# Attention layer: forming the second output tile ahead of the encoder's transposes in position 5

## The chip, the cores and the metric

The kernel runs on one core of a Trainium2 chip. The metric is the device time of one execution in microseconds (us), less is better.

## What is computed

The reference is two transformer blocks one after the other, all in float32, on x of shape (8, 256, 512). The first block ("first layer") is a cross-attention block over channels with its own feed-forward part. The second block is the one that matters here; cut to its core, for eight batches of 256 tokens and 512 features with 16 heads of 32:

```python
ln_out = layernorm(hidden_states, ln1_s, ln1_b)
q, k, v = split(ln_out @ w_qkv + b_qkv)
x = hidden_states + merge_heads(attention(q, k, v, ltor_mask)) @ w_ao + b_ao
ln_out = layernorm(x, ln2_s, ln2_b)
q = ln_out @ w_q + b_q
k, v = split(encoder_states @ w_kv + b_kv)
x = x + merge_heads(attention(q, k, v, cross_mask)) @ w_co + b_co
return x + gelu(layernorm(x, ln3_s, ln3_b) @ w1 + b1) @ w2 + b2
```

The eight self-attentions and the eight cross-attentions are done by `attention_layer` (lines 932 to 1892); the last line is `network_layer` (lines 1895 to 2340).

## The kernel before

`attention_layer` runs 16 rounds, v = 0 to 15: rounds 0 to 7 are the self-attention of batch 0 to 7, rounds 8 to 15 their cross-attention. A round has eight positions p = 0 to 7, one for each unit of four heads by 128 queries. The order of every engine is written out by hand: each has a function `position(v, p)` that runs in a loop over v and p, and the engines meet through semaphores alone (`Signal`, with `need` and `wait_ge`).

TensorE, position p of round v (L1484): the scores of the unit two ahead (L1446), the transposes of this unit's probabilities (L1458, two banks of four), in even positions the weighing of the values of two earlier units (L1475, then two transposes of the widened divisors, L1481), and at last `fill(v, p)`, the matmuls of other rounds that the table `FILL` lists for that position (L1395). Work that stands in `fill` and matters here, by its name in the table and its shift in rounds:

- ("o", n, -1): output tile n (128 tokens by 512) of the round before, a matmul of the bias (L1388) and twelve of 512 columns (L1391, `by_token`).
- ("enc", n, 2): half n of the encoder's transposes for round v + 2, four transposes into one bank (L1368, `turn`). It exists only where v + 2 is a cross round, so in the rounds v = 6 to 13.
- ("q", 0, 2) and ("k", 0, 2): the first halves of the queries and keys of round v + 2, 24 matmuls each (L1379, `project`), in positions 6 and 7. The keys wait for both low parts of the encoder (`enc_low`), the queries for the low part of the normalised input (`ln_low`).

All of this but the scores goes to six PSUM banks, `b_d`, in strict turn. The list `uses` (L1104 to L1118) holds every use of a bank in the order in which TensorE comes to them, with `FILL` read in its written order; use n lies in bank n mod 6. Before a use is written, `claim` (L1129) waits for the last reader of the use six places earlier, which had the same bank. The readers are: for "pt" the ACT copy (`pt_done`, L1617), for "w" the second DVE step of `divide` (`cx_done`, L1801), for "o" the DVE residual sum (`x_done`, L1819), for "enc" the second reader, DVE's `encoded_low` (`enc_low`, L1735).

In positions 5, 6 and 7 of rounds 6 to 13 the uses and the use whose bank each takes over are, before:

```
p5  pt, pt, enc 0 <- pt 4a, enc 1 <- pt 4b, o 1 <- w of p4
p6  pt <- o 0, pt, w, q 0 <- enc 0
p7  pt <- enc 1, pt <- o 1, k 0
```

VectorE (DVE), L1821: in each position first `soften` of the unit two ahead (the mask multiply L1777 and four minimum steps L1781), then in p5 `turned_low` (L1728) and `residual_sum` of tile 0, in p6 `residual_sum` of tile 1 and then `encoded_low`, two instructions of 128x512, then in even positions `divide` (L1799, L1801) and always the reciprocal (L1789). ScalarE (ACT), L1620: in p6 `context_high` (L1592), which waits for output tile 1 of the round before, and `encoded` (L1563), then in each position `keep` (L1617) and `exponentials` (L1605).

Three weights of the cross rounds are split in round 6: `WEIGHTS_AT` (L1153) puts 2 us of ACT and over 2 us of DVE work behind positions 1, 4 and 7 of that round.

Of the kernel before, what the change touches and what calls it, by code (L numbers as in the profile page):

```python
# [931 lines left out]
def attention_layer(nc, sems, hid, enc_in, masks, ident_in, W, mid_out, scratch):  # L932
# [55 lines left out]
    with ExitStack() as ctx:  # L988
        def sb(name, shape, dt=F32):
            return ctx.enter_context(nc.sbuf_tensor("b_" + name, shape, dt))  # L990

        def sig(name, per, unit=1):
# [6 lines left out]
        enc = sb("enc", [P, TT, D])  # L999
# [88 lines left out]
            2: [("v", 0, 1)],  # L1088
            3: [("v", 1, 1), ("turn", 0, 2), ("turn", 1, 2)],
            4: [("o", 0, -1)],  # L1090
            5: [("enc", 0, 2), ("enc", 1, 2), ("o", 1, -1)],
            6: [("q", 0, 2)],
            7: [("k", 0, 2)],
        }
# [1255 lines left out]
def build(nc, a, out):  # L2350
    x = a["x"]
    B, C, T = x.shape

    def scratch(name, shape, dt):
        return nc.dram_tensor(name, shape, dt, kind="Internal").ap()

    hid = scratch("hidden", [B, C, T], F32)
    mid = scratch("middle", [B, C, T], F32)


    with ExitStack() as sems:
        first_layer(nc, sems, x, a["ctx_2048"], a["positions"], a["identity"], {n: a["L0_xattn_" + n] for n in _L0}, hid,
                    scratch("a_q", [B, 3, C, T], BF16), scratch("a_k", [B, 3, C, T], BF16),
                    scratch("a_m", [B, 3, HEADS, T], BF16))
        W = {n: a["L1_xattn_" + n] for n in _L1}
        attention_layer(nc, sems, hid, a["ctx_2048"], (a["mask_1x1xSxS2_fc1"], a["mask_Bx1xSxS2_ff1"]), a["identity"],
                        W, mid, [[scratch(f"b_{n}{k}", [B, 2, T, C], F32) for n in "qk"] for k in range(2)])
        network_layer(nc, sems, mid, a["identity"], W, out)
# [35 lines left out]
```

How the kernel before makes its waits and increments, by code:

```python
    def need(self, eng, b, n):  # L31
        value = self.at(b, n)
        if not isinstance(value, int) or value > 0:
            eng.wait_ge(self.sem, value)
# [18 lines left out]
    def claim(self, eng, section, use, b, late=False):  # L54
        at = self.order[section].index(use)
        turn = section in ("peeled", "steady")
        if late and turn:
            b = b + 1
        if at >= self.n:
            before, batch = self.order[section][at - self.n], b
        elif section == "first":
            return self.bank(section, use)
        else:
            k = at % self.n
            order, batch = self.order["first" if section == "peeled" else "steady"], b - 1 if turn else b
            befores = [u for i, u in enumerate(order) if i % self.n == k]
            if not befores:
                return self.bank(section, use)
            before = befores[-1]
            turn = section != "peeled"
        signal, n, is_late = self.read[before]
        eng.wait_ge(signal.sem, signal.at(batch - 1 if is_late and turn else batch, n))
        return self.bank(section, use)
# [249 lines left out]
        def stored(eng, b):  # L326
            eng.wait_ge(o_out.sem, o_out.at(b, 1))
# [41 lines left out]
            def stack(b, g):  # L369
# [3 lines left out]
                exp_filled.need(sp, b - 1, (g + 1) * NP * TT)  # L373
                if b == 0 and g == 0:
                    sp.wait_ge(consts.sem, 1)
                pairs = slice(g * NP, (g + 1) * NP)
# [82 lines left out]
        @block.tensor  # L459
# [119 lines left out]
                    mm.then_inc(f2_filled.sem, 1)  # L579
            pe_.wait_ge(ident_here.sem, 16)
```

## Time and profile before

| | us |
|---|---|
| median of 3 runs | 1841.54 |
| lowest, highest | 1839.46, 1841.65 |
| the profiled execution, its own time | 1842.27 |
| its span, first to last instruction | 1840.5 |
| TensorE busy | 1717.6 (93%) |
| VectorE busy | 1207.0 (66%) |
| ScalarE busy | 1060.4 (58%) |
| mean granted TensorE clock | 0.959 of full |

The profile names each instruction by line, engine, output tile and input tiles. A wait is put down to the engine and line that released it. The granted clock of TensorE is 1.00 (2.4 GHz) or 0.50 (1.2 GHz) at any moment. The end of a matmul is modelled, so rows of matmuls that follow one another overlap by a fraction of a microsecond. The rounds 6 to 13 lie between about 1011 us and 1400 us of the span.

### The profile page before, as it was taken

What the parts mean: (1) busy time and instruction counts of PE and PEld (TensorE: products, weight loads), DVE (VectorE), ACT (ScalarE), POOL (GpSimd) and SP (SyncE); (2) the same over time, 40 slices, a digit from 0 to 9 for tenths busy, and PEclk for the clock granted to TensorE, in tenths of its full rate; (3) what the DMA queues carried; (4) which work ended last, traced back from release to release, by engine and by line L of the source; (5) the groups of instructions that cost most, each with busy time, mean ns of one, the idle gap of its engine ahead of it and who ended that gap; (6) DMA issues with size and microseconds to landing.
All of it is one profiled execution on the core that took longest, in us unless ns stands there. A gap on an engine that the chain in (4) does not pass through costs nothing.

```text
span 1840.5 us, 32546 instructions
## 1 busy us (share of the span) xinstructions
PE 1717.6 (93%) x11840; PEld 1233.4 (67%) x11840; DVE 1207.0 (66%) x2792; ACT 1060.4 (58%) x2333; POOL 142.4 (8%) x207
## 2 busy tenths in 40 slices
PE   3879999999999988999999999999999899999999
PEld 2424343444434333788889888888888789999998
DVE  5666776767776552588888888888888663333332
ACT  2345666756666564587788777777777631111111
POOL 2110101101000000000000000100000100000000
PEclk8779999999999898999999989999999999999999
DMA  6322223222222222567557757666666330000000
GB/s 161 111 86 67 94 82 100 71 93 88 83 71 68 80 61 87 152 157 182 153 156 200 198 163 200 169 173 173 167 167 168 116 121 25 25 25 25 25 26 13
DMA packets 169479, 201.62 MB, mean 110 GB/s; under 512 B 25956, under 2 KB 117220, under 8 KB 169320
## 3 DMA queue, kind: packets, MB, share of 16 engines
q1 hardware_dynamic: 169032, 199.14, 38.5%
q8 instruction: 95, 1.56, 0.4%
q10 hardware_dynamic: 288, 0.39, 0.2%
q14 instruction: 64, 0.52, 0.1%
HBM read 131.84 MB, written 67.63 MB: 108 GB/s over the span
## 4 chain that ended last, share of the span: by engine, by line
PE 81%; DVE 9%; ACT 5%; issue 2%; DVEq 1%; DMA 1%; ACTq 0%; POOL 0%; SPq 0%
PE c_d L2121 10%; PE b_d L1379 10%; PE c_sums L2136 10%; PE b_d L1391 9%; PE a_d L499 6%; PE b_d L1458 5%; PE a_escore L472 5%; PE a_d L569 3%; PE a_d L577 3%; PE a_mscore L484 3%; PE a_d L553 3%; PE b_score L1446 3%; PE b_d L1475 3%; DVE a_mx L802 2%; PE a_d L561 2%
## 5 line engine op out<-in xcount | busy, mean ns | idle before, releaser
L802 DVE TENSOR_REDUCE a_mx<-a_mscore 128x2 f32<-128x1024 f32 x247 | 302.3, 1224 | 171.8 <-PE a_mscore L484 170.2
L639 ACT ACTIVATE a_pt<-a_escore 128x1024 f32<-128x1024 f32 x256 | 262.5, 1025 | 165.1 <-PE a_escore L472 164.9
L1605 ACT ACTIVATE b_pr<-b_t,b_nmax 128x256 f32<-128x256 f32 x512 | 254.5, 501 | 121.4 <-DVE b_nmax L1781 121.0
L2220 ACT ACTIVATE c_gT<-c_d,c_b 128x256 f32<-128x256 f32 x128 | 53.7, 472 | 267.4 <-PE c_d L2121 267.4
L1777 DVE TENSOR_TENSOR b_t<-b_score,b_mask 128x1024 f32<-128x1024 f32 x128 | 155.0, 1211 | 75.6 <-PE b_score L1446 75.6
L1781 DVE CUSTOM_DVE_ANT_0 b_t<-b_t,b_minus 128x256 f32<-128x256 f32 x512 | 191.1, 429 | 16.9
L472 PEld LDWEIGHTS a_escore<-a_qst,a_kst 50*128 50x128 f32 x512 | 50.0, 191 | 180.4 <-ACT a_pt L639 109.6
L472 PE MATMUL a_escore<-a_qst,a_kst 50*128 50x512 f32 x512 | 133.8, 518 | 24.2 <-ACT a_pt L639 23.7
L2265 DVE CAST c_g_high<-c_gT 128x512 fp32r<-128x512 f32 x64 | 38.1, 595 | 172.0 <-ACT c_gT L2220 172.0
L2121 PE MATMUL c_d<-c_ln_high,c_w_high 128*128 128x256 f32 x512 | 145.4, 284 | 2.4 <-DVE c_ln_low L2267 2.4
L2121 PE MATMUL c_d<-c_ln_high,c_w_low 128*128 128x256 f32 x512 | 145.6, 284 | 0.0
L2121 PE MATMUL c_d<-c_ln_low,c_w_high 128*128 128x256 f32 x512 | 145.6, 284 | 0.0
L1458 PE MATMUL b_d<-b_ident,b_pr 128*128 128x128 f32 x1024 | 136.8, 277 | 4.9 <-DVE b_xr L1819 2.5
L1617 ACT ACTIVATE b_pt<-b_d 128x512 f32<-128x512 f32 x256 | 137.2, 590 | 4.5 <-PE b_d L1458 3.4
L484 PE MATMUL a_mscore<-a_kst,a_qst 48*128 48x512 f32 x494 | 113.0, 451 | 24.2 <-DVE a_mx L802 13.5
L499 PE MATMUL a_d<-a_pt,a_vaug 128*32 128x512 f32 x1024 | 131.2, 633 | 0.0
L1458 PEld LDWEIGHTS b_d<-b_ident,b_pr 128*128 128x128 f32 x1024 | 117.6, 143 | 6.1 <-DVE b_kparts L1752 3.1
L1379 PE MATMUL b_d<-b_lnp,b_wq 128*128 128x256 f32 x768 | 106.3, 298 | 15.5 <-DVE b_encp L1735 14.7
L1379 PEld LDWEIGHTS b_d<-b_lnp,b_wq 128*128 128x128 f32 x768 | 100.4, 203 | 18.6 <-issue 18.6
L2136 PE MATMUL c_sums<-c_w_high,c_g_high 128*128 128x512 f32 x256 | 102.0, 398 | 7.5 <-issue 6.7
L2121 PEld LDWEIGHTS c_d<-c_ln_high,c_w_high 128*128 128x128 f32 x512 | 98.8, 193 | 4.5 <-issue 2.6
L2136 PE MATMUL c_sums<-c_w_high,c_g_low 128*128 128x512 f32 x256 | 100.4, 392 | 0.0
(166 smaller groups left out, 3255.5 us busy)
## 6 DMA issues: line engine op xcount, KB each, us to landing
b_qst<-b_q SPq DMA_DIRECT2D x96, 256.0 KB, 4.7
b_kst<-b_k SPq DMA_DIRECT2D x96, 256.0 KB, 6.4
b_q<-b_qparts SPq DMA_DIRECT2D x64, 256.0 KB, 4.5
b_k<-b_kparts SPq DMA_DIRECT2D x64, 256.0 KB, 3.6
a_qst<-a_q_parts SPq DMA_DIRECT2D x192, 64.0 KB, 2.2
a_kst<-a_k_parts SPq DMA_DIRECT2D x186, 64.0 KB, 2.2
a_k_parts<-a_kparts SPq DMA_DIRECT2D x32, 256.0 KB, 2.3
a_q_parts<-a_qparts SPq DMA_DIRECT2D x32, 256.0 KB, 2.3
```

Of the source, the lines that this page charges most:

```text
L472: mm = nc.tensor.matmul(escore[:, e, :], kst[rows, pair, k * P:(k + 1) * P], qst[rows, pair, :], start=True, stop=True)
L484: mm = nc.tensor.matmul(maxima_bank(b, n)[:, e, :], qst[rows, pair, q * P:(q + 1) * P], kst[rows, pair, :], start=True, stop=True)
L499: mm = nc.tensor.matmul(at[32 * j:32 * j + 32, :], vaug[:, k, GROUP * g + j, :], pt[:, (b * UNITS + pair * TT + k) % RING, e, :], start=(k ...
L639: nc.scalar.activation(pt[:, at % RING, :, :], escore[:], ACT.Exp, scale=SCALE).then_inc(exp_done.sem, 1)
L802: nc.vector.tensor_reduce(mx[:, 2 * pair:2 * pair + 2, q], maxima_bank(b, n)[:], AX_X, ALU.max).then_inc(max_done.sem, 1)
L1379: mm = nc.tensor.matmul(at[:, j * S:(j + 1) * S], w[:, x, k, m:m + P], src[:, y, k, :], start=(k == 0 and c == 0), stop=(k == KT - 1 and c ...
L1391: mm = nc.tensor.matmul(at, src[:, x, k, n * P:(n + 1) * P], w[:, y, k, :], start=(k == 0 and c == 0 and not biased), stop=(k == KT - 1 an ...
L1458: last = nc.tensor.transpose(at[:, j * P:(j + 1) * P], pr[:, u % 2, j, k * P:(k + 1) * P], ident[:])
L1605: last = nc.scalar.activation(pr[:, u % 2, j, :], t[:, u % 2, j, :], ACT.Exp, scale=-1.0, bias=nmax[:, u, j:j + 1], accum_out=esum[:, u, j ...
L1781: last = nc.vector.tensor_tensor_reduce(t[:, u % 2, j, :], t[:, u % 2, j, :], minus[s][:, q, :], -1.0, HUGE, ALU.add, ALU.min, accum_out=n ...
L2121: mm = nc.tensor.matmul(bank[:, j * S:(j + 1) * S], w1[w][:, k, m:m + P], lnp[v][:, k, :], start=(k == 0 and n == 0), stop=(k == KT - 1 an ...
L2136: mm = nc.tensor.matmul(sums[:, t_, :], gp[v][:, u % RING, at:at + P], w2[:, row, :], start=(k == 0 and n == 0), stop=(k == FT - 1 and n = ...
```

## The change

In the table of fills, position 5, the entry of output tile 1 goes ahead of the two of the encoder's transposes. `uses` is built from the same table, so the banks of these uses change too.

```diff
@@ -1088,7 +1088,7 @@
             2: [("v", 0, 1)],
             3: [("v", 1, 1), ("turn", 0, 2), ("turn", 1, 2)],
             4: [("o", 0, -1)],
-            5: [("enc", 0, 2), ("enc", 1, 2), ("o", 1, -1)],
+            5: [("o", 1, -1), ("enc", 0, 2), ("enc", 1, 2)],
             6: [("q", 0, 2)],
             7: [("k", 0, 2)],
         }
```

After it, the same three positions read:

```
p5  pt, pt, o 1 <- pt 4a, enc 0 <- pt 4b, enc 1 <- w of p4
p6  pt <- o 0, pt, w, q 0 <- o 1
p7  pt <- enc 0, pt <- enc 1, k 0
```

## Rows read from the trace of the kernel before

**Rows 1.** The page's head and engines, and its chain by engine.
```profile
span 1840.5 us, 32546 instructions
...
PE 81%; DVE 9%; ACT 5%; issue 2%; DVEq 1%; DMA 1%; ACTq 0%; POOL 0%; SPq 0%
```
**Rows 2.** Waits, 1000 to 1390 us: total us, times, longest.
```profile
DVE b_t L1777 <- PE b_score L1446: 47.7, 40, 3.9
...
PE b_d L1379 <- DVE b_encp L1735: 14.7, 8, 2.1
...
PE b_d L1458 <- DVE b_xr L1819: 2.5, 1, 2.5
PE b_d L1458 <- DVE b_kparts L1752: 2.4, 2, 1.2
```
**Rows 3.** Timeline of TensorE, round 7: start, us, work, [idle before, releaser].
```profile
1100.09 1.04 PE L1368 MATMUL b_d<-b_ident,b_enc 128*128 128x128 f32 x8
...
1101.20 2.93 PE L1391 MATMUL b_d<-b_wo,b_cxp 128*128 128x512 f32 x12
...
1106.43 0.44 PE L1481 MATMUL b_d<-b_ident,b_wide 128*128 128x128 f32 x2
1108.82 3.10 PE L1379 MATMUL b_d<-b_lnp,b_wq 128*128 128x256 f32 x24 [1.96 <-DVE b_encp L1735]
...
1112.24 1.04 PE L1458 MATMUL b_d<-b_ident,b_pr 128*128 128x128 f32 x8
```
**Rows 4.** The chain that ended last, in order of time, the same place.
```profile
1107.47 0.60 DVE b_xr L1819
1108.08 0.61 DVE b_encp L1735
1108.69 0.14 issue
```
**Rows 5.** Timeline of TensorE, the queries of the rounds 6, 8, 9, 10 and 12.
```profile
1060.41 4.75 PE L1379 MATMUL b_d<-b_lnp,b_wq 128*128 128x256 f32 x24 [0.42 <-DVE b_encp L1735]
...
1152.49 4.60 PE L1379 MATMUL b_d<-b_lnp,b_wq 128*128 128x256 f32 x24 [2.06 <-DVE b_encp L1735]
...
1197.81 3.11 PE L1379 MATMUL b_d<-b_lnp,b_wq 128*128 128x256 f32 x24 [2.06 <-DVE b_encp L1735]
...
1241.49 4.60 PE L1379 MATMUL b_d<-b_lnp,b_wq 128*128 128x256 f32 x24 [2.06 <-DVE b_encp L1735]
...
1330.27 4.62 PE L1379 MATMUL b_d<-b_lnp,b_wq 128*128 128x256 f32 x24 [2.06 <-DVE b_encp L1735]
```
**Rows 6.** Busy by stretch: us, PE, PEld, DVE, ACT, POOL busy, granted clock, DMA share, GB/s.
```profile
1109.00:1111.00 2.00, 2.00 (x18) 2.00 (x18) 1.11 (x4) 0.58 (x3) 0.29 (x1) 1.00 1.05 380
1153.00:1155.00 2.00, 2.00 (x11) 2.00 (x11) 1.55 (x4) 2.00 (x4) 0.73 (x1) 0.50 0.55 205
...
1078.00:1080.00 2.00, 2.00 (x11) 2.00 (x10) 1.87 (x4) 2.00 (x8) 0.29 (x1) 0.50 0.79 256
```
**Rows 7.** Timeline of TensorE: position 1 of round 7, and a later wait.
```profile
1075.22 0.74 PE L1446 MATMUL b_score<-b_kst,b_qst 96*128 96x256 f32 x4 [0.24 <-DVE b_t L1777]
...
1077.62 1.00 PE L1458 MATMUL b_d<-b_ident,b_pr 128*128 128x128 f32 x4 [1.21 <-DVE b_kparts L1752]
1078.27 4.42 PE L1379 MATMUL b_d<-b_encp,b_wk 128*128 128x256 f32 x24
...
1425.76 0.71 PE L1446 MATMUL b_score<-b_kst,b_qst 96*128 96x256 f32 x4 [1.37 <-DVE b_t L1777]
```
**Rows 8.** Timelines of ACT and DVE in round 7: the readers of the banks.
```profile
1096.94 1.09 ACT L1617 ACTIVATE b_pt<-b_d 128x512 f32<-128x512 f32 x2
...
1105.07 1.06 ACT L1563 ACTIVATE b_encp<-b_d 128x512 fp32r<-128x512 f32 x2
...
1098.03 0.42 DVE L1801 TENSOR_TENSOR b_cx<-b_d,b_spread 128x256 f32<-128x256 f32 x1
```
**Rows 9.** Timeline of DVE in round 6: the residual sum in position 6.
```profile
1058.97 0.69 DVE L1819 TENSOR_TENSOR b_xr<-b_d,b_xr 128x512 f32<-128x512 f32 x1
```

## The prediction

> **What bounds the kernel now.** I read the page's chain first: TensorE holds 81% of a span of 1840.5 us [rows 1]. The change touches only the rounds that have encoder transposes, 6 to 13. There the list of waits says where TensorE still stands idle: 14.7 us before the first half of the queries, once in each of eight rounds, released by DVE's `encoded_low`; the next largest of its waits on DVE are 2.5 us and 2.4 us in all, in rounds 6 and 7, where weights are split [rows 2]. DVE on the other hand waits for TensorE's scores 40 times, 47.7 us in all [rows 2]: in most positions TensorE leads the whole, and a microsecond less of it is a microsecond less of time.
>
> The timeline of round 7 shows the place. Position 5 runs the encoder's eight transposes at 1100.09, then output tile 1. Position 6 ends with the widened divisors at 1106.43 + 0.44 = 1106.87, and the queries start only at 1108.82, after 1.96 us of idleness [rows 3]. Why they wait is in the table of banks: the queries take over the bank of encoder half 0, whose last reader is `encoded_low`. The chain gives the order on DVE to a hundredth: residual sum of tile 1 until 1108.08, then 0.61 us of the first `encoded_low`, 0.14 us of issue, then the queries [rows 4].
>
> **Second, the clock.** The queries last 3.10 to 3.11 us in rounds 7, 9, 11 and 13, and 4.60, 4.60 and 4.62 us in rounds 8, 10 and 12, after the same idleness of 1.96 to 2.06 us [rows 3, 5] (rounds 11 and 13 repeat the row of round 9, with 2.06 and 3.10). The granted clock says why: 1.00 in 1109 to 1111 us, 0.50 in 1153 to 1155 us [rows 6], which is the level of 1.2 GHz instead of 2.4 GHz. The fall comes as the wait ends, in three of seven such rounds, and costs 1.50 + 1.50 + 1.52 = 4.5 us.
>
> **The change part by part.**
>
> *Moved: thirteen matmuls ahead of eight transposes.* The same instructions run in position 5, so its length on TensorE stays: 0. No DMA and no queue entry of SP or POOL is moved. The transfer of the next encoder input waits for the transposes, which now end some 3 us later. SP comes to it only in the next round, behind the store of the first query half that TensorE has not even begun then, so: 0.
>
> *Claims of position 5.* Output tile 1 now takes the bank of the first probability copy of position 4. ACT starts that pair of copies at 1096.94 and ends it by 1098.03 against a need at 1100.09. Encoder half 1 takes the bank that `divide` reads until 1098.45 [rows 8], needed only some 3.5 us after 1100.09. Cover of 2 us or more: 0. If it were gone, TensorE would stand by the lateness.
>
> *Claim of the queries.* It now asks for `x_done`, not for the first `enc_low`. DVE's own order is untouched, and the residual sum stands directly ahead of `encoded_low`, so the queries can start one `encoded_low` earlier: 0.61 us [rows 4], not the whole 1.96. The wait is shortened, not removed; the residual sum, behind the softening of the same position, is what is late next. Its operands don't hold it either: `ln_low` came in position 5. In round 6 only 0.42 us of idleness stands before the queries [rows 5], and the residual sum ends at 1058.97 + 0.69 = 1059.66 [rows 9], ahead of TensorE's arrival (1060.41 - 0.42 = 1059.99): all 0.42 us goes. Sum: 7 x 0.61 + 0.42 = 4.7 us.
>
> *Claims of position 7.* The two probability transposes now take the banks of encoder halves 0 and 1. The second `encoded_low` ends near 1108.08 + 2 x 0.61 = 1109.3; TensorE arrives at 1112.24 - 0.61 = 1111.6 [rows 3, 4]. Cover 2.3 us: 0. The keys waited for both low parts already.
>
> *ACT.* `encoded` needs the transposes, now the last work of position 5. They end where tile 1 ended before, near 1101.20 + 2.93 = 1104.1 [rows 3]; ACT reaches them at 1105.07 [rows 8], since `context_high`, which needed tile 1, comes first. 0.9 us of cover: 0.
>
> *The clock.* The idleness falls from 1.96 to 2.06 us to 1.35 to 1.45 us. No row of before shows exactly that in this place. Bounds: the three falls all go, -4.5 us; or all seven rounds fall, +4 x 1.50 = +6.0 us. The nearest rows speak both ways: a wait of 1.37 us at 1425.76 left the matmuls behind it at full speed, while one of 1.21 us at 1077.62, shortly behind a pause of 0.24 us, was followed by 0.50 and keys of 4.42 us [rows 6, 7]. I take -4.5, because in this same place, with the same work around it, even 1.96 to 2.06 us left the clock alone in four rounds of seven: a wait 30% shorter should be on the safe side in all.
>
> The Trainium skill, "TensorE: Matmul & The Clock Gate", section "HAM oscillation", gives as a rule an idle gap that must not be exceeded if the clock is to stay; every wait here, before and after, is shorter than the gap it names. By that rule the clock would play no part and the sum would be -4.7 us; the falls after 2.06 us show that the rule is too lenient for this place.
>
> Sum: -4.7 - 4.5 = -9.2 us. The profiled execution took 1842.27 us, which gives 1833.1; it lies 0.7 above the median of the runs shown, 1841.54, and against that the forecast is **1832.3 us** (-0.50%). After round 13 nothing takes it back that I can see: the later waits for weights and stores start from events of these rounds and shift along.
>
> **Rivals.**
>
> *A. Only the wait shrinks.* The clock falls as often as before, since where it falls hangs on more than the length of one wait. For: the 1.21 us wait with its fall. Against: the four undisturbed rounds at 2 us. -4.7: 1836.8.
>
> *B. More clock comes back.* In round 6 the clock was low from the weighing on, and the queries took 4.75 us instead of 3.10 with a pause of 0.42 us before them. If it recovers sooner once that pause is gone, 1.6 us more is saved; if the fall at 1077.62 then also misses its place, the keys there get 4.42 - 3.10 = 1.3 us back. -9.2 - 2.9 = -12.1: 1829.4.
>
> *C. The wait is not the bank's.* If the last thing the queries wait for were something behind `encoded_low` or the wait returned in position 7, nothing would be gained: -0, 1841.5. Against: the chain ties the start to the first `encoded_low` to 0.14 us, and position 7 has 2.3 us of cover.
>
> *D. Slower: the shortened wait falls on the clock every time.* The mechanism is one: idleness near 1.4 us, shifted against what precedes it, makes the clock fall at the queries of all seven rounds. Price: +6.0 - 4.7 = +1.3 us, 1842.8. If each low stretch in addition cost as much as round 6's queries (1.65 instead of 1.50 us) and the following keys of position 7 were caught too, at 1.3 us each as in [rows 7], it would be 7 x 2.95 - 4.5 - 4.7 = +11.5 us, 1853.0. It decides if a wait of 1.4 us does more than one of 2 us did in four of seven rounds; only the row of 1.21 us speaks for it.
>
> **How the numbers follow.** A measurement of this kernel can tell about 0.2%, 3.7 us, from no change. Forecast 55%, A 24%, B 12%, C 5%, D 4%. The range reaches from a little below B, 1829.0, to a little above A, 1837.6 (A with a fall more than before), and leaves out C, D and the tails. Faster by over 0.2% means under 1837.9: the forecast, B and five sixths of A make 0.87; the rest of A, C and half of D make 0.10; slower by over 0.2%, the far half of D and what I have not thought of: 0.03.
>
> **What would show it.** In rounds 7 to 13 the queries' row should have an idle of 1.3 to 1.5 us, put down to the residual sum, L1819, and last 3.10 us each; `encoded_low` should no longer release TensorE anywhere; eight transposes should follow tile 1 in position 5. Queries of 4.6 us in some rounds speak for A, in all for D; a recovery near 1061 us for B. A wait at L1458 in position 7, or at L1563 on ACT behind the transposes, would make the sum wrong, and so would an idle that stays at 2 us.

## The result, and the profile after

| | before | after |
|---|---|---|
| median, us | 1841.34 (6 runs) | 1830.69 (6 runs) |
| lowest to highest | 1839.46 to 1844.91 | 1828.64 to 1831.62 |
| profiled execution, its own time | 1842.27 | 1830.12 |
| its span | 1840.5 | 1828.3 |

The ratio after to before is 0.994, with a 95% interval of 0.9927 to 0.9953: 10.65 us less, where 9.2 us were forecast. The mean granted clock says the same of all six executions of the changed kernel: it lies between 0.961 and 0.965, against 0.957 to 0.961 in the 27 executions of the kernel before that were taken beside the first four experiments.

The page after, its head and its chain by engine, against [rows 1]:

```profile
span 1828.3 us, 32546 instructions
...
PE 79%; DVE 10%; ACT 6%; issue 3%; DVEq 1%; DMA 1%; ACTq 0%; POOL 0%; SPq 0%
```

The number of instructions is the same, and TensorE still holds the chain, with two points less.

The waits in 1000 to 1390 us, after (engine and line, what released it: total us, times, longest), against [rows 2]:

```profile
DVE b_t L1777 <- PE b_score L1446: 38.1, 39, 2.2
...
PE b_d L1379 <- DVE b_xr L1819: 10.1, 7, 1.5
...
PE b_d L1458 <- DVE b_kparts L1752: 3.0, 3, 1.2
...
PE b_d L1458 <- DVE b_xr L1819: 2.5, 1, 2.5
```

`encoded_low` (L1735) releases TensorE nowhere any more. Its place ahead of the queries is taken by the residual sum (L1819), seven times instead of eight, and 14.7 us have become 10.1. That is the wait that was shortened, not removed.

Round 7 on TensorE, after (start, us, work, idle before it), against [rows 3]:

```profile
1096.53 2.93 PE L1391 MATMUL b_d<-b_wo,b_cxp 128*128 128x512 f32 x12
1099.30 1.03 PE L1368 MATMUL b_d<-b_ident,b_enc 128*128 128x128 f32 x8
...
1102.62 0.44 PE L1481 MATMUL b_d<-b_ident,b_wide 128*128 128x128 f32 x2
1104.42 3.11 PE L1379 MATMUL b_d<-b_lnp,b_wq 128*128 128x256 f32 x24 [1.36 <-DVE b_xr L1819]
```

The transposes now follow the twelve matmuls of tile 1, and the idleness is 1.36 us against 1.96. The chain of the same execution shows what is left of it, against [rows 4]:

```profile
1103.67 0.61 DVE b_xr L1819
1104.29 0.14 issue
1104.42 3.11 PE b_d L1379 x24
```

The 0.61 us of `encoded_low` are gone from the chain; the issue of 0.14 us stayed. The rounds 8 to 13 repeat one row, with 3.10 or 3.11 us and an idle of 1.46 (first and last of the six):

```profile
1147.50 3.11 PE L1379 MATMUL b_d<-b_lnp,b_wq 128*128 128x256 f32 x24 [1.46 <-DVE b_xr L1819]
...
1362.99 3.11 PE L1379 MATMUL b_d<-b_lnp,b_wq 128*128 128x256 f32 x24 [1.46 <-DVE b_xr L1819]
```

No queries of 4.6 us are left [rows 5]. The row of the stretch in round 8 has the granted clock in its third column from the right, 1.00 now against 0.50 in [rows 6]:

```profile
1148.00:1150.00 2.00, 2.00 (x19) 2.00 (x19) 1.55 (x5) 2.00 (x6) 0.12 (x1) 1.00 0.69 262
```

Rounds 6 and 7 changed in a way that I had only as a rival:

```profile
1055.73 1.94 PE L1475 MATMUL b_d<-b_pt,b_val 128*32 128x128 f32 x32
1057.60 0.69 PE L1481 MATMUL b_d<-b_ident,b_wide 128*128 128x128 f32 x2
1058.13 3.55 PE L1379 MATMUL b_d<-b_lnp,b_wq 128*128 128x256 f32 x24
...
1074.16 0.66 PE L1458 MATMUL b_d<-b_ident,b_pr 128*128 128x128 f32 x4 [1.21 <-DVE b_kparts L1752]
1074.57 3.12 PE L1379 MATMUL b_d<-b_encp,b_wk 128*128 128x256 f32 x24
...
1084.70 0.66 PE L1458 MATMUL b_d<-b_ident,b_pr 128*128 128x128 f32 x4 [0.59 <-DVE b_kparts L1752]
```

The clock is still low at the weighing of round 6 (1.94 us), but the queries take 3.55 us instead of 4.75, with no pause before them. The keys of round 7 take 3.12 us instead of 4.42 after the same wait of 1.21 us [rows 7]. And there is a new wait, of 0.59 us at 1084.70.

**Where the time came from**, by how much earlier the same instruction starts in the profile after than in that before:

| point | before | after | earlier by | gained since |
|---|---|---|---|---|
| round 6, probabilities of position 6 | 1056.41 | 1054.73 | 1.68 | |
| round 6, scores after the queries | 1064.99 | 1061.52 | 3.47 | 1.79 |
| round 7, scores of position 5 | 1098.74 | 1094.94 | 3.80 | 0.33 |
| round 7, queries | 1108.82 | 1104.42 | 4.40 | 0.60 |
| round 13, queries | 1375.45 | 1362.99 | 12.46 | 8.06 |
| end of the span | 1840.5 | 1828.3 | 12.2 | -0.3 |

The change begins in position 5 of round 6, just ahead of the first point of the table. The last work before it, the probabilities of that position, starts at 1048.55 and 1046.89, so 1.66 of the first 1.68 us are a difference between two executions. Stretches at a granted clock of 0.50 in the first 1000 us add up to 109.2 us in the profile before and 102.4 in that after, so the profile before came late into these rounds; the change has no part in that. 12.2 - 1.7 = 10.5 us are left, which agrees with the medians.

### The profile page after: what moved, and what is told of

Same layout as the page of the kernel before. It is cut to its first block, busy times and chain, and to the rows that moved or that the text cites. A ratio compares the mean times of both kernels' runs of the same rounds, so it can differ in the third digit from the quotient of the medians.

```text
span 1828.3 us, 32546 instructions
## 1 busy us (share of the span) xinstructions
PE 1708.0 (93%) x11840; PEld 1224.9 (67%) x11840; DVE 1206.6 (66%) x2792; ACT 1060.2 (58%) x2333; POOL 142.2 (8%) x207
## 4 chain that ended last, share of the span: by engine, by line
PE 79%; DVE 10%; ACT 6%; issue 3%; DVEq 1%; DMA 1%; ACTq 0%; POOL 0%; SPq 0%
PE c_d L2121 10%; PE c_sums L2136 10%; PE b_d L1379 8%; PE b_d L1391 8%; PE a_d L499 6%; PE a_escore L472 5%; PE b_d L1458 5%; PE a_d L569 3%; PE a_d L577 3%; PE a_mscore L484 3%; PE a_d L553 3%; PE b_score L1446 3%; PE b_d L1475 2%; DVE a_mx L802 2%; DVE b_t L1781 2%
## 5 line engine op out<-in xcount | busy, mean ns | idle before, releaser
L484 PE MATMUL a_mscore<-a_kst,a_qst 48*128 48x512 f32 x494 | 112.4, 449 | 23.9 <-DVE a_mx L802 13.7
L1379 PE MATMUL b_d<-b_lnp,b_wq 128*128 128x256 f32 x768 | 100.7, 287 | 10.9 <-DVE b_xr L1819 10.1
L1379 PEld LDWEIGHTS b_d<-b_lnp,b_wq 128*128 128x128 f32 x768 | 94.8, 192 | 13.8 <-issue 13.8
```

Of the source, the lines that this page charges most:

```text
L484: mm = nc.tensor.matmul(maxima_bank(b, n)[:, e, :], qst[rows, pair, q * P:(q + 1) * P], kst[rows, pair, :], start=True, stop=True)
L1379: mm = nc.tensor.matmul(at[:, j * S:(j + 1) * S], w[:, x, k, m:m + P], src[:, y, k, :], start=(k == 0 and c == 0), stop=(k == KT - 1 and c ...
```

## The experiments

The theory: the queries wait for the last reader of the bank that they take over, that reader's place in VectorE's order sets the length of the wait, and the length of the wait decides whether the clock falls behind it. The rivals: it is the order on TensorE that helps (tile 1 is ready a microsecond earlier), or the falls of the clock are a matter of phase (where in time a wait lies) and not of the wait's length.

Each set of experiments was timed beside the kernel before: 1840.56 us (27 runs) for the first four, 1840.20 (9 runs) for the next two, 1840.63 (9 runs) for the last two. The ratios are against these. They lie up to 1.1 us under the 1841.34 of the result, so a microsecond between medians of different sets says nothing.

**Banks alone.** The order of TensorE's work as before, the banks as after:

```diff
-                uses += [(name, v + shift, n) for name, n, shift in FILL[p] if has(name, v + shift)]
+                names = FILL[p] if p != 5 else [FILL[5][2], FILL[5][0], FILL[5][1]]
+                uses += [(name, v + shift, n) for name, n, shift in names if has(name, v + shift)]
```

> Banks as after the change, order of TensorE's work as before it. Theory (what counts is whose bank the queries take over): as the changed kernel, 1830.7 us (1829 to 1832.5), idle before the queries 1.36 to 1.46 us in rounds 7 to 13, released by the residual sum, no low clock there. Rival (what counts is that tile 1 is ready a microsecond earlier): as before, 1841.3 us, with the idle at 2.06 us.

Measured: 1830.77 us (1828.6 to 1833.55, 5 runs), ratio to before 0.9947 (0.9934 to 0.9959). Its line numbers are one higher; round 7 on TensorE:

```profile
1094.68 1.04 PE L1369 MATMUL b_d<-b_ident,b_enc 128*128 128x128 f32 x8
...
1095.79 2.92 PE L1392 MATMUL b_d<-b_wo,b_cxp 128*128 128x512 f32 x12
```

```profile
1102.80 3.11 PE L1380 MATMUL b_d<-b_lnp,b_wq 128*128 128x256 f32 x24 [1.36 <-DVE b_xr L1820]
```

The transposes are ahead of tile 1 again, and the wait is 1.36 us all the same. The whole effect is there: 9.8 us against the kernel before of the same set, where the change gave 10.65 against its own, with intervals of some 2 us each.

**Order alone.** The order as after, the banks as before (the same two lines in the changed kernel, with `[FILL[5][1], FILL[5][2], FILL[5][0]]`):

> Order as after the change, banks as before it. Theory: the queries again wait for the first low part of the encoder, idle 2.06 us, two to four queries at half clock, 1841.3 us (1839 to 1843). Rival (the order counts): 1830.7 us.

Measured: 1841.01 us (1838.61 to 1842.06, 11 runs), ratio 1.0002 (0.9993 to 1.0011). The queries of rounds 7 and 8:

```profile
1105.27 3.10 PE L1380 MATMUL b_d<-b_lnp,b_wq 128*128 128x256 f32 x24 [1.96 <-DVE b_encp L1736]
...
1148.95 4.59 PE L1380 MATMUL b_d<-b_lnp,b_wq 128*128 128x256 f32 x24 [2.06 <-DVE b_encp L1736]
```

Rounds 8, 10 and 12 are at half clock as before. The two runs settle the first rival: TensorE's order by itself is worth nothing that they can show (the interval is about 1.7 us to either side), the hand-over of the banks is worth all that they can show.

**One low part first.** The changed kernel, with the wait given back its old length:

```diff
                 if p == 6:
+                    encoded_low(v + 2, (0,))
                     residual_sum(v - 1, 1)
-                    encoded_low(v + 2)
+                    encoded_low(v + 2, (1,))
```

> The changed kernel with the first low part of the encoder put ahead of the residual sum on VectorE, 0.68 us more for the queries to wait for, nothing else changed. Theory (the length of the wait sets the clock): idle back at 2.06 us, queries of 4.6 us in two to four of the seven rounds, 1830.7 + 7 x 0.61 + 0.42 + 4.5 = 1839.8 us, plus up to 2 us if round 6 also loses its earlier recovery: 1838 to 1842. Rival (the new order keeps the clock up whatever the wait): no queries of 4.6 us, 1830.7 + 4.7 = 1835.4 us.

Measured: 1840.75 us (1839.16 to 1842.51, 11 runs), ratio 1.0 (0.9991 to 1.0008). The queries of rounds 6, 7, 8 and 10:

```profile
1058.35 4.73 PE L1379 MATMUL b_d<-b_lnp,b_wq 128*128 128x256 f32 x24 [0.38 <-DVE b_xr L1819]
...
1106.76 3.10 PE L1379 MATMUL b_d<-b_lnp,b_wq 128*128 128x256 f32 x24 [1.96 <-DVE b_xr L1819]
...
1150.43 4.60 PE L1379 MATMUL b_d<-b_lnp,b_wq 128*128 128x256 f32 x24 [2.06 <-DVE b_xr L1819]
...
1239.43 4.61 PE L1379 MATMUL b_d<-b_lnp,b_wq 128*128 128x256 f32 x24 [2.06 <-DVE b_xr L1819]
```

Here `encoded_low` stands between the softening and the residual sum, the new reader. With the new order and the new banks, 0.6 us more of waiting brought the old profile back: 2.06 us, queries of 4.6 us in rounds 8, 10 and 12, and 4.73 us in round 6. The rival of a protected clock (1835.4 us) is out. The rival of phase is not: this kernel runs the rounds at nearly the times of the one before, so the two can't be told apart here.

**Both low parts first.** The same lines, with `encoded_low(v + 2)` whole ahead of the residual sum:

> The changed kernel with both low parts of the encoder ahead of the residual sum. Theory: idle 1.46 + 1.28 = 2.7 us in rounds 7 to 13, which is 8 x 1.28 - 0.4 = 9.8 us more than the changed kernel, and the clock falls in more rounds than before, four to seven at 1.5 us each: 1830.7 + 9.8 + 6.0 to 10.5 = 1846.5 to 1851 us. Rival (the clock falls are luck of the phase, about three of seven whatever the wait): 1830.7 + 9.8 + 4.5 = 1845.0 us, with three falls.

Measured: 1844.61 us (1842.55 to 1846.57, 11 runs), ratio 1.0022 (1.0013 to 1.0031). The queries of rounds 8, 9, 10 and 13:

```profile
1152.22 5.46 PE L1379 MATMUL b_d<-b_lnp,b_wq 128*128 128x256 f32 x24 [2.65 <-DVE b_xr L1819]
...
1199.28 4.58 PE L1379 MATMUL b_d<-b_lnp,b_wq 128*128 128x256 f32 x24 [2.65 <-DVE b_xr L1819]
...
1245.04 3.10 PE L1379 MATMUL b_d<-b_lnp,b_wq 128*128 128x256 f32 x24 [2.65 <-DVE b_xr L1819]
...
1377.84 3.10 PE L1379 MATMUL b_d<-b_lnp,b_wq 128*128 128x256 f32 x24 [2.65 <-DVE b_xr L1819]
```

This is a miss of the theory. The wait grew as expected, by 1.2 us, but the clock fell in two rounds of seven and not in four or more. Against the changed kernel the rows give 7 x 1.2 = 8.4 us of waiting, 5.46 + 4.58 - 2 x 3.10 = 3.8 us of clock and some 1.9 us in round 6 (0.99 us of pause, queries of 4.48): 14.1, measured 13.9. In this profiled execution the longer wait did not make the falls more frequent. The rival held that phase decides, with about three falls and 1845.0 us; it has the time better than the theory, but its three falls are not met either.

**Residual sum early.** The changed kernel, with what the queries still wait for moved ahead of the softening on VectorE:

```diff
                 if p == 5:
                     turned_low(v + 2)
                     residual_sum(v - 1, 0)
+                    residual_sum(v - 1, 1)
                 if p == 6:
-                    residual_sum(v - 1, 1)
                     encoded_low(v + 2)
```

> The changed kernel with the second residual sum at the end of position 5 on VectorE, ahead of the softening of position 6. Tile 1 is filled by then in the new order. Theory (the residual sum behind the softening is all that the queries still wait for): no idle before them, 1830.7 - 1.36 - 6 x 1.46 = 1820.6 us; up to 2 us may come back where VectorE is then late: 1820 to 1823. Rival (another wait stands right behind, so that the wait only changes its releaser): 1828 us or more, with an idle of over 1 us before the queries or in position 7.

Measured: 1819.47 us (1818.08 to 1820.15, 4 runs), ratio 0.9885 (0.987 to 0.990). VectorE and TensorE in round 7:

```profile
1098.89 1.28 DVE L1819 TENSOR_TENSOR b_xr<-b_d,b_xr 128x512 f32<-128x512 f32 x2
```

```profile
1102.00 0.44 PE L1481 MATMUL b_d<-b_ident,b_wide 128*128 128x128 f32 x2
1102.20 3.11 PE L1379 MATMUL b_d<-b_lnp,b_wq 128*128 128x256 f32 x24
```

The queries follow without idleness. All of 1.36 + 6 x 1.46 = 10.1 us was to be had. Against 1830.69 the median is 11.2 us lower, half a microsecond under the range expected; against the kernel before of its own set the gain is 20.7 us, 10.1 more than the 10.65 of the change.

**The same move in the kernel before.** The diff above, applied to the old table:

> The kernel before, with the second residual sum at the end of position 5. The queries wait for the first low part of the encoder, which now comes straight behind the softening. Theory: the same release as in the changed kernel, idle 1.4 us, no low clock in rounds 7 to 13, 1830.7 us (1829 to 1833); tile 1 is finished 0.9 us later in this order, so VectorE may wait for it in position 5, some tenths a round. Rival (only the order or the banks help): 1841.3 us.

Measured: 1832.88 us (1831.7 to 1834.58, 5 runs), ratio 0.996 (0.9947 to 0.9972). The queries of rounds 8, 11 and 12:

```profile
1150.18 3.11 PE L1379 MATMUL b_d<-b_lnp,b_wq 128*128 128x256 f32 x24 [1.62 <-DVE b_encp L1735]
...
1280.01 4.48 PE L1379 MATMUL b_d<-b_lnp,b_wq 128*128 128x256 f32 x24 [1.62 <-DVE b_encp L1735]
...
1324.75 3.11 PE L1379 MATMUL b_d<-b_lnp,b_wq 128*128 128x256 f32 x24 [1.62 <-DVE b_encp L1735]
```

The wait is 1.62 us here, since tile 1 comes last in position 5 and VectorE meets it 0.2 us too early. It gains most of what the change gained, and one round of seven still falls to half clock, where none was expected.

**Round 6 late.** The changed kernel, with one low part first in round 6 alone:

```diff
                 if p == 6:
+                    if v == B - 2:
+                        encoded_low(v + 2, (0,))
                     residual_sum(v - 1, 1)
-                    encoded_low(v + 2)
+                    encoded_low(v + 2, (1,) if v == B - 2 else (0, 1))
```

> The changed kernel with the first low part of the encoder ahead of the residual sum in round 6 alone. Theory (the pause of 0.4 us before the queries of round 6 is what keeps the clock low for 6.8 instead of 3.4 us): pause back at 0.4 us, queries of round 6 at 4.7 us instead of 3.55, rounds 7 to 13 as changed, 1830.7 + 0.4 + 1.2 + 0.3 for what follows in round 7 = 1832.5 us (1831.5 to 1833.5). Rival (round 6 recovered earlier by chance of the run): queries of 3.55 us or a mixture, 1831.1 us.

Measured: 1831.03 us (1829.76 to 1831.75, 5 runs), ratio 0.9947 (0.9934 to 0.9959). Round 6's queries and round 7's keys of position 1:

```profile
1059.54 4.83 PE L1379 MATMUL b_d<-b_lnp,b_wq 128*128 128x256 f32 x24 [0.45 <-DVE b_xr L1819]
...
1077.42 4.47 PE L1379 MATMUL b_d<-b_encp,b_wk 128*128 128x256 f32 x24
```

In the rows the theory holds: with a pause of 0.45 us the queries are back at 4.83 us, and the fall at the keys returned as well. The queries of round 7 start 3.03 us later than in the changed kernel's profile (1107.45 against 1104.42). Of this 0.90 us was there at the queries of round 5, before the edit acts, so some 2.1 us were lost, and at the queries of round 13 the distance is still 3.00 us. At the end of the span it is 0.9 us. The stretches at a granted clock of 0.50 between 1400 and 1500 us add up to 10.2 us in this profile, against 17.1 in the changed kernel's, so the loss was given back there; whether that is a rule or chance, one profile can't say. Nor can the medians: the 1.8 us expected on top of 1830.7 did not come, but against the kernel before of its own set the gain is 9.6 us, 1.05 less than the change's, and the intervals are wider than the question.

**Weights later.** The kernel with the residual sum early, and VectorE's half of the weight splits of rounds 6 to 8 one position behind ScalarE's:

```diff
-                if (v, p) in WEIGHTS_AT:
-                    low_weight(WEIGHTS_AT[v, p])
+                at = (v, p) if v < B - 2 else divmod(v * NU + p - 1, NU)
+                if at in WEIGHTS_AT:
+                    low_weight(WEIGHTS_AT[at])
```

> The second residual sum at the end of position 5, as in the faster run, and VectorE's half of the weight splits of rounds 6 to 8 one position later than ScalarE's. VectorE no longer waits 2.5 us for ScalarE in position 4 of round 6. Theory (the waits of 1.2, 2.5, 1.2 and 0.6 us of rounds 6 and 7 and the low clock behind two of them come from the splits): 1819.5 less up to 2.5 + 1.2 and 1.7 us for each of the two low stretches that goes, 1813 to 1817 us. Rival (VectorE is full there, so the split only stalls another position): 1818 us or more.

Measured: 1812.51 us (1811.91 to 1814.29, 5 runs), ratio 0.9846 (0.9832 to 0.9859); 7.0 us below the kernel without it (7.4 by the gains against the kernel before of each set), half a microsecond under the range expected. Some of what is left of the waits in rounds 6 and 7:

```profile
1052.21 1.06 PE L1458 MATMUL b_d<-b_ident,b_pr 128*128 128x128 f32 x8 [0.61 <-DVE b_xr L1819]
...
1054.41 3.12 PE L1379 MATMUL b_d<-b_lnp,b_wq 128*128 128x256 f32 x24
...
1058.47 1.16 PE L1458 MATMUL b_d<-b_ident,b_pr 128*128 128x128 f32 x8 [0.47 <-DVE b_encp L1735]
```

The wait of 2.5 us is down to 0.61 and the queries of round 6 run at full clock. No stretch between 1000 and 1390 us is at 0.50 any more; the changed kernel still had 6.8 us of it there, the kernel before 23.9:

```profile
1000.00:1390.00 390.00, 383.11 (x3626) 345.08 (x3626) 344.26 (x1053) 317.67 (x942) 32.30 (x83) 1.00 0.71 186
```

Other waits came in or grew, and cost less: the 0.47 us above, 1.24 us ahead of output tile 0 in round 6 (1042.71), and in position 3 of round 7 1.00 us where it was 0.59.

## Why the prediction was right, and where not

*The claim of the queries.* Right to the hundredth: 0.60 us in round 7 (1.96 to 1.36) and 0.60 us in the six rounds after it (2.06 to 1.46), against 0.61; in round 6 all 0.42 us went. "Banks alone" and "Order alone" show that the mechanism is the one given, the residual sum in place of `encoded_low` as the reader of the bank, and "Residual sum early" that nothing else stood close behind it.

*The clock.* The value taken, all three falls gone for 4.5 us, is what came: the queries of rounds 8, 10 and 12 went from 4.6 to 3.1 us. Together the steps for rounds 7 to 13 were 7 x 0.61 + 4.5 = 8.8 us; the table above has 0.60 + 8.06 = 8.7. "One low part first" shows that the falls come back when the wait does. The reason given, that a wait 30% shorter was on the safe side, was right in the outcome but does not hold in general: "Both low parts first" had a longer wait and fewer falls. So there was some luck in taking all of the 4.5 us.

*Costs put at nothing.* The order of position 5, the new claims of its three uses, the claims of position 7 and the encoder's copy on ACT each showed no wait in the profile after, as forecast.

*What the sum left out.* Round 6. Its queries recovered the clock sooner, as rival B had it for 1.6 us beyond the pause; the profile has 1.79 us with the pause, so 1.4 us for the clock. That step of the sum, "all 0.42 us goes", was mis-sized: it counted the pause and not what the pause does to the clock. Of rival B's second part, 1.3 us at the keys of round 7, the keys did get it: the scores behind them start at 1077.53 instead of 1082.52, 4.99 us earlier, where the row of the table ahead has 3.47. But only 0.33 us of these 1.5 was left 20 us later. The chain after shows why:

```profile
1068.13 0.99 DVE b_wv L1700
...
1083.86 0.80 DVE b_kparts L1752 x2
1084.66 0.05 issue
1084.70 0.66 PE b_d L1458 x4
```

From the weight split, which waits for ScalarE until 1068.13, to the new wait of 0.59 us the chain runs through VectorE. There the prediction's opening thought, that in most positions a microsecond less of TensorE is a microsecond less of time, does not hold. So B came true by about half, with 10.65 us against 9.2 for the forecast and 12.1 for B. Since the median of "Round 6 late" can't confirm the 1.8 us, how much of the last 1.4 us of the result belongs to round 6, and how much to the runs' spread of about 3 us, stays open.

*The rivals.* Of their chances one sum is off by a hundredth: the rest of A, C and half of D make 0.11, not 0.10. A would have shown queries of 4.6 us; there are none. C and D asked for no gain or more falls; the profile has neither.

*"After round 13 nothing takes it back."* Nearly: 0.3 us were taken back. The longest waits there are the same (2.04 and 2.11 us, for the softening), the one of 1.37 us between them grew to 1.52, and the low stretches only moved.

The rule that the prediction cites from the Trainium skill, "TensorE: Matmul & The Clock Gate", section "HAM oscillation", would put the clock term at zero. The measurement decides for 4.5 us.

## What to carry to other kernels

Where work takes PSUM banks in strict turn, the order of the list does two things, it sets what TensorE does first and whose bank each use inherits; look at the second, and at where the last reader of that bank stands in its own engine's order. When such a wait is only shortened, move its new releaser next: here that was worth as much again as the change, for one line moved. A repeated idle of one or two microseconds on TensorE should be priced with the clock behind it, which here doubled its worth (4.5 us of clock beside 4.2 of waiting in rounds 7 to 13).

## What the runs showed of the hardware

Waits before the queries of rounds 7 to 13 and queries at half clock, over the profiled executions: 1.36 to 1.46 us, none of 21 (changed kernel, "Banks alone", "Round 6 late"); 1.54 to 1.62 us, one of 7; 1.96 to 2.06 us, nine of 21 (before, "Order alone", "One low part first", each in rounds 8, 10 and 12); 2.56 to 2.65 us, two of 7. The shortest waits had no fall here, but the longest had fewer than the middle ones. The counts are smaller than they look: each kernel has one profile, and the three with the old wait run these rounds at nearly the same distances, so their nine falls are one pattern seen three times. That the same three rounds fell each time suggests that where in time a wait lies counts as well as its length; this was not tried by itself.

In round 6 the clock is low before the queries come. There a pause of 0.38 to 0.47 us before them went with queries of 4.7 to 4.8 us in all five kernels that had it, and no pause with 3.55, 3.49 and 3.6 us in the changed kernel, "Banks alone" and "Residual sum early". The low stretch lasted 6.8 us with a pause (also with the 0.99 us of "Both low parts first") and 3.4 us without. "Round 6 late" differs from the changed kernel in nothing but VectorE's order in that round, so the pause, or the later start that comes with it, is the cause. The granted clock of the stretches behind it, of "Round 6 late" and of the changed kernel:

```profile
1061.00:1063.00 2.00, 2.00 (x11) 2.00 (x11) 0.00 (x0) 0.00 (x0) 0.27 (x1) 0.50 0.37 133
```

```profile
1059.00:1061.00 2.00, 2.00 (x18) 2.00 (x18) 1.02 (x4) 0.64 (x4) 0.29 (x1) 0.97 0.66 245
```

They begin 1.5 and 0.9 us after the start of the queries; the first is at 0.50 throughout, the second at 0.97. A wait of 1.21 us in position 1 of round 7 was followed by a fall in the kernel before [rows 7] and by none in the changed kernel, at 1074.16. So one and the same length of wait can do either.
